# Attention and expert layer: the turn of each result over four steps, and the value products in quarters around the raw scores

## The reference, cut to what matters

```python
x  = L0_attn_x                                # (8, 1024, 128) float32
xn = _layernorm(x)
# attention on xn: 8 heads, dqk = 2, dv = 16
scores = einsum('bmhd,bnhd->bhmn', q, k) / sqrt(dqk)
scores = where(scores >= 0, scores, 0.2 * scores)
beta   = softmax(scores, axis=-1)
out    = einsum('bhmn,bnhd->bmhd', beta, v)
attn   = gamma * out + xn
# ffn on xn: 16 experts (1 zero, 1 copy, 2 constant, 12 MLP), top 2 per token, capacity 1024
x = x + attn + ffn
```

## Time and profile before

| | us |
|---|---|
| median of 2 executions | 1056.45 (1056.41 to 1056.5) |
| the profiled execution's own time | 1051.31 |
| its span, first to last instruction | 1049.5 |
| TensorE matmuls busy | 899.8 (86%) |
| DVE busy | 776.2 (74%) |
| ACT busy | 694.1 (66%) |
| POOL busy | 578.6 (55%) |

### The profile page before, as it was taken

The page is one execution under the profiler, slowest core; times in us unless marked ns, Lnnn a source line. Parts: engine busy times, 40 slices in busy tenths (PEclk is TensorE's granted clock), DMA queues, the critical chain, the costliest instruction groups (busy, mean ns, idle before and its releaser), DMA issues.

```text
span 1049.5 us, 20085 instructions
## 1 busy us (share of the span) xinstructions
PE 899.8 (86%) x7619; PEld 367.1 (35%) x7620; DVE 776.2 (74%) x915; ACT 694.1 (66%) x803; POOL 578.6 (55%) x591
## 2 busy tenths in 40 slices
PE   0777612999999999999899999989999999999997
PEld 0444300222222222222377777752222222222222
DVE  6799986899998999899600000028999899989995
ACT  0566620778887878788754544447788877887885
POOL 2455523660373274076199998007754774774776
PEclk9987855899999999999999999999999999999999
DMA  8611100010010000001223323411102112102000
GB/s 217 246 47 46 46 13 24 29 41 2 26 43 16 17 32 22 13 15 33 68 71 125 105 86 121 126 52 28 32 12 68 28 28 61 28 18 58 13 28 25
DMA packets 48159, 55.29 MB, mean 53 GB/s; under 512 B 10714, under 2 KB 35122, under 8 KB 48080
## 3 DMA queue, kind: packets, MB, share of 16 engines
q1 hardware_dynamic: 39888, 44.84, 14.1%
q0 software_dynamic: 8192, 9.37, 3.0%
HBM read 31.57 MB, written 30.02 MB: 59 GB/s over the span
## 4 chain that ended last, share of the span: by engine, by line
PE 64%; DVE 13%; issue 8%; ACT 6%; POOL 5%; SPq 2%; DMA 1%; DVEq 1%; POOLq 0%; ACTq 0%
PE ps L732 19%; PE ps L712 12%; PE ps L702 11%; PE ps L790 8%; PE ps L782 8%; DVE ps L1002 6%; ACT pr L605 3%; POOL xs L444 2%; PE ps L656 2%; PE ps L742 2%; ACT ot L597 2%; PE ps L660 1%; POOL y L462 1%; SPq L248 1%; DVE xs L863 1%
## 5 line engine op out<-in xcount | busy, mean ns | idle before, releaser
L605 ACT ACTIVATE pr<-ps 128x1024 f32<-128x1024 f32 x512 | 523.2, 1024 | 164.9 <-PE ps L712 124.8
L1002 DVE TENSOR_SCALAR ps<-ps 128x1024 f32<-128x1024 f32 x512 | 601.2, 1225 | 13.8 <-PE ps L702 11.0
L732 PE MATMUL ps<-pr,vp 128*32 128x256 f32 x4096 | 328.5, 393 | 0.3
L712 PE MATMUL ps<-q,kz 64*128 64x512 bf16 x1024 | 201.8, 391 | 46.3 <-DVE ps L1002 46.2
L702 PE MATMUL ps<-q,kz 62*128 62x512 bf16 x1024 | 201.3, 390 | 12.3 <-ACT pr L605 8.4
L444 POOL DMA_INDIRECT xs<-eout,idxs x128 | 128.8, 1007 | 55.4 <-issue 32.8
L427 POOL DMA_INDIRECT disp<-xs,idxs x128 | 125.7, 982 | 46.5 <-issue 39.4
L712 PEld LDWEIGHTS ps<-q,kz 64*128 64x128 bf16 x1024 | 49.3, 93 | 263.9 <-DVE ps L1002 223.5
L1016 DVE TENSOR_TENSOR pr<-ps,parts 128x1024 f32<-128x1024 f32 x12 | 14.7, 1225 | 165.6 <-PE ps L790 165.6
L732 PEld LDWEIGHTS ps<-pr,vp 128*32 128x32 f32 x4096 | 81.4, 108 | 128.5 <-issue 126.2
L413 POOL TENSOR_TENSOR y<-y,att 128x256 f32<-128x256 f32 x32 | 23.1, 725 | 184.2 <-DVE att L990 178.6
(11 more groups left out here) (120 smaller groups left out, 655.7 us busy)
## 6 DMA issues: line engine op xcount, KB each, us to landing
disp<-pr SPq DMA_DIRECT2D x12, 512.0 KB, 5.0
eout<-pr SPq DMA_DIRECT2D x12, 512.0 KB, 3.0
y<-in_x SPq DMA_DIRECT2D x8, 512.0 KB, 7.2
out<-y SPq DMA_DIRECT2D x8, 512.0 KB, 3.3
w<-in_w1t SPq DMA_DIRECT2D x12, 256.0 KB, 3.2
w<-in_w2t SPq DMA_DIRECT2D x12, 256.0 KB, 3.4
xs<-disp SPq DMA_DIRECT2D x6, 512.0 KB, 5.2
pr<-disp SPq DMA_DIRECT2D x6, 512.0 KB, 4.9
```

The costliest lines, as they stand in the source:

```text
L605: act.activation(pr[:, c % BUFS, 2 * pair:2 * pair + 2, :], ring[i % RING], ACT.Exp, scale=SLOPE).then_inc(S["exps"], 1)
L712: last = pe.matmul(ring[i % RING][:, k, :], kz[r:r + TILE, hg, pair, kc * P:(kc + 1) * P], q2[r:r + TILE, hg, qh * HALF:(qh + 1) * HALF], ...
L732: last = pe.matmul(acc[p % 2][32 * g:32 * g + 32, cols], vp[:, hg, kc, g, :], pr[:, c % BUFS, g % PAIRS * 2 + g // PAIRS, cols], start=(kc ...
L1002: dve.tensor_scalar(s, s, 0.0, 1.0 / SLOPE - 1.0, ALU.max, ALU.mult).then_inc(S["relu"], 1)
```

## The change

`values` takes a quarter of 128 queries instead of a half of 256, so that a step makes two calls of it instead of one. The first comes right behind `shifted(i)`, ahead of `scores(i + 2)`; the second at the old place. `turn` makes one transpose per call, at steps 6, 7, 8 and 9, between the scores and the second quarter. DVE's `denominators` moves from ahead of step 7 to ahead of step 12, and `finish` from behind the `tensor_scalar` of step 7 to ahead of that of step 13.

```diff
-DENOM = 7
+DENOM = 12
+FINISH = 13
...
-            def values(c, half):
+            def values(c, quarter):
...
-                cols = slice(half * HALF // 2, (half + 1) * HALF // 2)
+                cols = slice(quarter * P, (quarter + 1) * P)
                 pe.wait_ge(S["exps"], PAIRS * (c + 1))
...
-                if half:
+                if quarter == 3:
                     last.then_inc(S["pv"], 1)
...
-            def turn(p):
-                pe.wait_ge(S["acc_evac"], p + 1)
-                for t in range(GT):
-                    last = pe.transpose(acc[p % 2][:, t * P:(t + 1) * P], ot[:, p % 2, t * P:(t + 1) * P], ident)
-                last.then_inc(S["o_rdy"], 1)
+            def turn(p, t):
+                if t == 0:
+                    pe.wait_ge(S["acc_evac"], p + 1)
+                last = pe.transpose(acc[p % 2][:, t * P:(t + 1) * P], ot[:, p % 2, t * P:(t + 1) * P], ident)
+                if t == GT - 1:
+                    last.then_inc(S["o_rdy"], 1)
...
                     shifted(i)
+                    if i > first + PAIRS:
+                        values((i - 3) // PAIRS, (i - 3) % PAIRS * 2)
                     if i + AHEAD < end:
                         scores(i + AHEAD)
-                    if i % UP == TURN and i > first + UP:
-                        turn(i // UP - 1)
+                    if 0 <= i % UP - TURN < GT and i > first + UP:
+                        turn(i // UP - 1, i % UP - TURN)
                     if i > first + PAIRS:
-                        values((i - 3) // PAIRS, (i - 3) % PAIRS)
+                        values((i - 3) // PAIRS, (i - 3) % PAIRS * 2 + 1)
                 for j in range(end - 3, end):
-                    values(j // PAIRS, j % PAIRS)
-                turn(end // UP - 1)
+                    for k in range(2):
+                        values(j // PAIRS, j % PAIRS * 2 + k)
+                for t in range(GT):
+                    turn(end // UP - 1, t)
...
                     if done is not None and i % UP == DENOM:
                         denominators(done)
+                    if done is not None and i % UP == FINISH:
+                        finish(done)
                     dve.wait_ge(S["s1"], i + 1)
                     s = ring[i % RING]
                     dve.tensor_scalar(s, s, 0.0, 1.0 / SLOPE - 1.0, ALU.max, ALU.mult).then_inc(S["relu"], 1)
-                    if done is not None and i % UP == DENOM:
-                        finish(done)
```

More of the change, by code:

```diff
@@ L715, in shifted @@
                 last.then_inc(S["s2"], 1)
-            def values(c, half):
+            def values(c, quarter):
                 p, kc = divmod(c, TB)
                 hg = p // NQ % NHG
-                cols = slice(half * HALF // 2, (half + 1) * HALF // 2)
+                cols = slice(quarter * P, (quarter + 1) * P)
                 pe.wait_ge(S["exps"], PAIRS * (c + 1))
-                if kc == 0 and half == 0:
+                if kc == 0 and quarter == 0:
                     if p == 0:
@@ L733, in values @@
                                      pr[:, c % BUFS, g % PAIRS * 2 + g // PAIRS, cols],
-                                     start=(kc == 0 and half == 0), stop=(kc == TB - 1), tile_position=(0, 32 * g),
+                                     start=(kc == 0 and quarter == 0), stop=(kc == TB - 1), tile_position=(0, 32 * g),
                                      skip_group_check=True)
-                if half:
+                if quarter == 3:
                     last.then_inc(S["pv"], 1)
-            def turn(p):
-                pe.wait_ge(S["acc_evac"], p + 1)
-                for t in range(GT):
-                    last = pe.transpose(acc[p % 2][:, t * P:(t + 1) * P], ot[:, p % 2, t * P:(t + 1) * P], ident)
-                last.then_inc(S["o_rdy"], 1)
+            def turn(p, t):
[4 more added lines that the diff above has]
+                    last.then_inc(S["o_rdy"], 1)
             def attention(b0):
```

## The result

| | before | after |
|---|---|---|
| median of 2 executions, us | 1056.45 | 1109.37 (1109.18 to 1109.55) |
| ratio, with its 95% interval | | 1.0501 (1.0456 to 1.0546) |
| span of the profiled execution, us | 1049.5 | 1107.4 |
| one pass, between copies of accumulators, us | 21.11 | 22.72 |

Forecast: 1112 us, 80% range 1080 to 1145.

The account below looks back on a forecast made before the run. Before, steps of 1.20 us were set by a loop through ACT, plus a 1.91 us turn; after, TensorE bounds. Terms +50.7, +4.2 and +0.3, about +55 us, on the 1056.45 median gave 1112 us, 80% range 1080 to 1145.

Parts of the forecast that it names:

- The bound and the step: In the attentions, TensorE bounds every step without waits; a step takes 1.36 us instead of 1.20.
- A quarter at 0.36: A value product of 128 queries takes 0.14 us to its second round plus 0.22 to the next tile.
- The transposes: In four steps of a pass a lone transpose adds 0.26 us, 1.04 a pass, against 0.58 for the row.
- The turn's wait: DVE's 64.1 us idle before its reciprocals go; on the path worth 1.91 us a pass less the transposes' time.
- The cover: In the second attention POOL's later chain still ends 2.1 us before it is needed; shorter passes would lose this.
- The sum: Both attentions together: +50.7 us for 30 passes with a turn, +4.2 first passes, +0.3 ends, about +55 us.
- rival 1: In the attentions switching is hidden and DVE bounds at 1.13 us a step; POOL delays the second; 1014 us; chance 0.07.
- rival 2: Short products in the attentions switch more cheaply, step 1.27 us, transpose 0.20; gain and loss cancel, 1060 us; chance 0.08.
- rival 3: TensorE's 40 matmuls and weight loads a step come out too slowly, step 1.45 to 1.6 us; 1157 at 1.45; chance 0.11.

Follow-up runs that it names:

- the fourth experiment: The kernel before the change with only DVE's reciprocal and scaling moved to steps 12 and 13, transposes still in one row: 1041.21 us, ratio 0.9851.

## Why the prediction was right

**The bound and the step.** TensorE was forecast as the bound with no waits and a step of 1.36; both are in the trace, and 318.08 busy of 318.08 us is as plain as such a row gets.

**A quarter at 0.36.** The size held, its parts did not. In the quarter that begins at 511.32 the second round starts at 511.45 and the next tile at 511.68: 0.13 and 0.23 us, where I had 0.14 and 0.22. The weights held nothing up. With both quarters behind the scores the four rounds start at 301.94, 302.08, 302.19 and 302.30: behind the first gap a round adds only 0.11, about its streaming. I had given each short round an overhead, and the second its weights' 0.01 too, so I expected 1.16 for TensorE there, and it was 1.11. The whole extra, 1.36 against 1.11, belongs to the changes of tile: 0.12 us each where I had put 0.08 to 0.09, and 0.10 with nothing but a tiny product between. One size was too high and one too low, so the right sum is in part luck; that the changes of tile make the step, and not the columns or the count, is what the experiments bear out.

The Trainium skill (TensorEngine Tiling (Array Packing), section Key Properties) says that a change of tiling mode drains TensorE. These runs agree that each change has a price, 0.10 to 0.12 us, and that load and product both wait for it; that draining is what takes the time they do not show.

**The transposes.** 0.26 for a lone one was read from the row of four and measured as 0.26. The pass was forecast at 22.80 and is 22.72, 16 x 1.355 + 4 x 0.26.

**The turn's wait.** DVE's 64.1 us were forecast to go; they fell to 8.1, those of the two last turns. On the path they were put at 1.91 us less the transposes' own 0.58, that is 1.33 a pass. DVE's move alone gave 1.16 with halves (21.11 to 19.96) and 1.29 with quarters (23.57 to 22.28), a little less than forecast. In the change the quarters' loss outweighs this gain. With whole halves it is 3% of the time once the scaling is early enough for POOL.

**POOL.** The cover was forecast at 2.1 us. POOL's last additions before the end and the one that waits for the last pass:

```profile
1100.29 1.41 POOL L414 TENSOR_TENSOR y<-y,att 128x256 f32<-128x256 f32 x2
...
1103.02 0.72 POOL L414 TENSOR_TENSOR y<-y,att 128x256 f32<-128x256 f32 x1 [1.32 <-DVE att L996]
```

The two end at 1101.70 and the last begins at 1103.02: 1.3 us. The condition, that shorter passes would lose it, came true in the fourth experiment: from the end of the last transpose to the end of the span are 12.4 us there, against 5.2 before. The late values, which cost more, stood in the prediction under rival 1 alone.

**The sum.** Forecast +55 us; the attentions give 45.0 + 8.2, some 53. I added it to the median (1056.45) and not to the profiled execution (1051.31), and came out 2.6 us above the measured 1109.37; the other way would have been 1106, some 3 below. Nothing here says that one was right: with a prologue that varies by 7 us between traces, a hit this close is luck.

**The rivals.** That switching is hidden (rival 1) and that short products switch more cheaply (rival 2) fell with the 0.32 and 0.36 starts. That 40 matmuls and loads a step come out too slowly (rival 3) fell with both quarters together, which ran them in 1.11 us, one per 28 ns, with no wait for weights.

## What to carry to other kernels

Count the changes of tile in a loop of packed matmuls, not the instructions: products of one tile next to each other are nearly free to cut (down to the 128 columns tried here), while each change costs about the same, 0.10 to 0.12 us, whether the products beside it stream 1, 128 or 256 columns. When a change consists of two edits, run each alone: here one gained 1.4% and hid behind the other's 7% loss. And a consumer moved to take away a wait should move only as far as the wait asks, since another engine's chain may hang on it: steps 8 and 9 gave twice what steps 12 and 13 gave.

## What the runs showed of the hardware that I had not expected

A matmul of one column in the value products' tile costs 0.20 us between products of another tile (0.32 + 0.11 against 0.23) and 0.01 beside one of its own. At a change of tile neither the product nor its weight load begins early. And in a wait of 3.6 us on TensorE in the middle of an attention the granted clock fell, and it was 0.50 from 947 to 951.4 us, when TensorE was busy again, so a wait there cost up to 5.5 us (25.42 against 19.96 for the pass).
